# Low-rank products of four sequences at a time, with high halves and rests stacked in 128 rows

## The reference, cut to what matters

```python
# cond: B = 32 sequences, T = 32 tokens, rank R = 16
base_out = jnp.einsum('bti,oi->bto', x, W) + b
A = lora_As[adapter_mapping]          # per sequence: 512 x 16
Bm = lora_Bs[adapter_mapping]         # per sequence: 16 x 512
lora_h = jnp.einsum('bti,bir->btr', x, A)
lora_out = jnp.einsum('btr,bro->bto', lora_h, Bm)
xt = base_out + lora_out * 2.0
# ffn: router (softmax, 2 of 16 experts within 2 of 4 groups), experts, shared expert
y = sum over experts e: gate[:, e] * ((silu(xt @ w1 + b1) * (xt @ w2 + b2)) @ w3 + b3)
z = silu(xt @ sw1 + sb1) * (xt @ sw2 + sb2) @ sw3 + sb3
out = x + y + z
```

## Time and profile before

| | |
|---|---|
| median of three runs | 129.47 us (129.31 to 129.48) |
| profiled execution, its own time | 129.17 us |
| its span, first to last instruction | 127.3 us |
| mean granted TensorE clock | 1.000 |
| TensorE matmuls busy (815 instructions) | 123.3 us |
| TensorE weight loads busy (815) | 102.0 us |
| VectorE busy (195) | 86.4 us |
| ScalarE busy (84) | 47.8 us |

### The profile page before, as it was taken

One profiled execution on the slowest core, in us unless ns is written; L12 is line 12 of the kernel. 1 busy time (PEld: TensorE's weight loads), 2 busy tenths in 40 slices (PEclk: granted clock), 3 DMA queues, 4 the chain that ended last, 5 costly groups with the idle time before them and its releaser, 6 DMA issues.

```text
span 127.3 us, 2241 instructions
## 1 busy us (share of the span) xinstructions
PE 123.3 (97%) x815; PEld 102.0 (80%) x815; DVE 86.4 (68%) x195; ACT 47.8 (38%) x84; POOL 19.0 (15%) x33
## 2 busy tenths in 40 slices
PE   6999999999999999999999999999999999999991
PEld 6978867987789787888788889886888888888891
DVE  1659194257879859989999964456715379997631
ACT  1644473697529644007654654241014010000000
POOL 7364005000000020000057000033800000000000
PEclk9999999999999999999999999999999999999999
DMA  3999788669990699549007999994227999332222
GB/s 109 298 322 399 241 351 257 261 221 376 376 346 14 122 192 227 122 143 345 6 0 194 364 278 397 392 359 161 94 82 250 347 396 369 124 127 103 99 88 82
DMA packets 16908, 28.77 MB, mean 226 GB/s; under 512 B 1952, under 2 KB 6432, under 8 KB 16768
## 3 DMA queue, kind: packets, MB, share of 16 engines
q1 hardware_dynamic: 11728, 17.07, 40.5%
q10 hardware_dynamic: 3952, 7.34, 15.9%
q0 software_dynamic: 1216, 4.20, 10.3%
HBM read 19.17 MB, written 9.44 MB: 225 GB/s over the span
## 4 chain that ended last, share of the span: by engine, by line
PE 84%; DMA 6%; SPq 5%; ACT 2%; issue 1%; DVE 0%; ACTq 0%
PE bank L1002 61%; DMA xT_raw<-in_xT 6%; PE bank L1204 6%; PE bank L1061 5%; PE bank L1218 3%; SPq L319 2%; PE bank L1049 2%; PE bank L1279 2%; PE bank L1072 1%; PE bank L1194 1%; PE bank L1035 1%; ACT xT_h L462 1%; PE bank L1109 1%; PE bank L1179 1%; SPq L327 1%
## 5 line engine op out<-in xcount | busy, mean ns | idle before, releaser
L1002 PE MATMUL bank<-xtT_h,w12e_h 128*128 128x512 f32 x32 | 13.1, 409 | 0.0
L1002 PE MATMUL bank<-xtT_h,sw_h 128*128 128x512 f32 x32 | 12.9, 403 | 0.0
L1002 PE MATMUL bank<-xtT_l,sw_h 128*128 128x512 f32 x32 | 12.5, 391 | 0.0
L1002 PE MATMUL bank<-xtT_l,w12e_h 128*128 128x512 f32 x32 | 12.5, 391 | 0.0
L1002 PE MATMUL bank<-xtT_h,w12e_l 128*128 128x512 f32 x32 | 12.5, 391 | 0.0
L1002 PE MATMUL bank<-xtT_h,sw_l 128*128 128x512 f32 x32 | 12.5, 390 | 0.0
L975 DVE SCALAR_TENSOR_TENSOR x_sb<-rows_sb,val,x_sb 128x512 f32<-128x512 f32 x16 | 11.7, 747 | 0.2
L981 DVE TENSOR_TENSOR x_sb<-x_sb,bank 128x512 f32<-128x512 f32 (+1 forms) x9 | 5.6, 625 | 4.8 <-PE bank L1002 4.8
L799 DVE SCALAR_TENSOR_TENSOR heT_sb<-bank,b_dense,sg_sb 128x512 f32<-128x512 f32 x4 | 3.0, 750 | 7.7 <-PE bank L1002 7.7
L1204 PEld LDWEIGHTS bank<-xgT_sb,w_ring 128*128 128x128 f32 x64 | 7.5, 192 | 0.5 <-issue 0.5
L678 DVE TENSOR_TENSOR xT_l<-xT_raw,xT_h 128x512 fp32r<-128x512 f32 (+1 forms) x6 | 5.2, 867 | 3.9 <-ACT xT_h L462 3.8
(11 more groups left out here) (185 smaller groups left out, 292.0 us busy)
## 6 DMA issues: line engine op xcount, KB each, us to landing
y_rows<-zeros ACTq DMA_DIRECT2D x2, 2048.0 KB, 10.6
rows_sb<-y_rows SPq DMA_DIRECT2D x8, 512.0 KB, 7.3
xT_raw<-in_xT SPq DMA_DIRECT2D x8, 256.0 KB, 6.9
xt_rows<-xt_turned SPq DMA_DIRECT2D x8, 256.0 KB, 4.8
w_ring<-in_w_turned SPq DMA_DIRECT2D x4, 512.0 KB, 9.2
x_sb<-in_x SPq DMA_DIRECT2D x1, 2048.0 KB, 14.8
out<-x_sb ACTq DMA_DIRECT2D x7, 256.0 KB, 2.0
condW_raw<-in_condWT ACTq DMA_DIRECT2D x4, 256.0 KB, 5.1
```

The lines of the kernel that those rows point to most:

```text
L1002: mm = pe.matmul(out, a[p], b[q], start=(start and n == 0), stop=(stop and n == 2))
```

## The change

Each group is cut in two halves `h` of four sequences: 64 rank rows and 128 tokens. In `loraB_stack[:, g % 2, h]` the 64 rows of the half hold B's high half, and the other 64 rows hold its rest. `lhT_twice` holds the high half of the masked product in both sets of rows, `lhT_rest` the rest in the own rows, with zeros in the others. So one matmul over 128 rows gives high by high plus rest by high, and a second one gives the high by rest: two matmuls of 128 moving tokens for each half, four for a group and chunk, where three of 256 were.

The copies and rests of B are made for each half, in 64 partitions each (the rests written to the other 64 partitions). The mask has 128 columns (`lmask_half`, added up from `lmask` once); VectorE copies the high half to the own rows, ScalarE to the others (`move_lhT`), VectorE makes the rests. ScalarE's and VectorE's work on groups 0 and 1 of B is moved ahead of x's second half. GpSimd's gathers wait for the same work, counted in halves.

```diff
-        lhT_split = at(162, "lhT_h", [P, 2, GT], F32R), at(164, "lhT_l", [P, 2, GT], F32R)
-        loraB_split = at(168, "loraB_h", [P, 2, DIM], F32R), at(172, "loraB_l", [P, 2, DIM], F32R)
+        lhT_twice = at(162, "lhT_twice", [P, 2, 2, P], F32R)
+        lhT_rest = at(164, "lhT_rest", [P, 2, 2, P], F32R)
+        loraB_stack = at(168, "loraB_stack", [P, 2, 2, DIM], F32R)
...
# GpSimd, gather_lora
-                    pool.wait_ge(loraB_done, g - 1)
+                    pool.wait_ge(loraB_done, 2 * (g - 1))
...
# ScalarE, hi_loraB and hi_lhT (now move_lhT)
-                act.copy(loraB_split[0][:, g % 2], lora_raw[:, g % 2, DIM:2 * DIM]).then_inc(loraB_hi, 1)
+                for h, rows in enumerate(ROW_HALVES):
+                    act.copy(loraB_stack[rows, g % 2, h], lora_raw[rows, g % 2, DIM:2 * DIM]).then_inc(loraB_hi, 1)
...
-                act.copy(lhT_split[0][:, g % 2], lhT_sb[:]).then_inc(lhT_hi, 1)
+                for h, rows in enumerate(ROW_HALVES):
+                    act.copy(lhT_twice[ROW_HALVES[1 - h], g % 2, h], lhT_sb[rows, 0:P]).then_inc(lhT_moved, 1)
...
# ScalarE, order
+            hi_loraB(0)
+            hi_loraB(1)
             hi_xT(1, 0, 2)
             hi_xT(1, 2, 4)
-            hi_loraB(0)
             copy_loraA(0)
-            hi_loraB(1)
             copy_loraA(1)
-            hi_lhT(0)
-            hi_lhT(1)
+            move_lhT(0)
+            move_lhT(1)
...
# VectorE
             dve.memset(lhT_sb[:, 0:P], 0.0).then_inc(zeros_ready, 1)
+            then(dve.memset(lhT_rest[:].bitcast(F32), 0.0))
...
-                dve.wait_ge(loraB_hi, g + 1)
-                rest(loraB_split[1][:, g % 2], lora_raw[:, g % 2, DIM:2 * DIM], loraB_split[0][:, g % 2], loraB_done)
+                for h, rows in enumerate(ROW_HALVES):
+                    dve.wait_ge(loraB_hi, 2 * g + h + 1)
+                    rest(loraB_stack[ROW_HALVES[1 - h], g % 2, h], lora_raw[rows, g % 2, DIM:2 * DIM],
+                         loraB_stack[rows, g % 2, h], loraB_done)
...
# VectorE, mask_lh
                 if g >= 1:
-                    dve.wait_ge(lhT_done, g)
+                    dve.wait_ge(lhT_done, 2 * g)
+                    dve.wait_ge(lhT_moved, 2 * g)
                 dve.wait_ge(lh_done, g + 1)
-                quarters = "p (q t) -> p q t"
-                dve.tensor_tensor(lhT_sb[:].rearrange(quarters, q=QUARTER),
-                                  bank[5][:, 0:P // 2].unsqueeze(1).to_broadcast([P, QUARTER, P // 2]),
-                                  lmask[:].rearrange("p q r -> p (q r)").rearrange(quarters, q=QUARTER), ALU.mult
+                halves = "p (q t) -> p q t"
+                dve.tensor_tensor(lhT_sb[:, 0:P].rearrange(halves, q=2),
+                                  bank[5][:, 0:HALF_P].unsqueeze(1).to_broadcast([P, 2, HALF_P]),
+                                  lmask_half[:].rearrange("p q r -> p (q r)").rearrange(halves, q=2), ALU.mult
                                   ).then_inc(lh_masked, 1)
-                dve.wait_ge(lhT_hi, g + 1)
-                rest(lhT_split[1][:, g % 2], lhT_sb[:], lhT_split[0][:, g % 2], lhT_done)
+                if g >= 2:
+                    dve.wait_ge(cond_done, KC)
+                dve.wait_ge(lh_masked, g + 1)
+                for h, rows in enumerate(ROW_HALVES):
+                    dve.tensor_copy(lhT_twice[rows, g % 2, h], lhT_sb[rows, 0:P]).then_inc(lhT_hi, 1)
+                for h, rows in enumerate(ROW_HALVES):
+                    dve.wait_ge(lhT_hi, 2 * g + h + 1)
+                    rest(lhT_rest[rows, g % 2, h], lhT_sb[rows, 0:P], lhT_twice[rows, g % 2, h], lhT_done)
...
# VectorE, order
+            lo_lora(0)
+            lo_lora(1)
             lo_xT(1, 0, 2)
             lo_xT(1, 2, 4)
-            lo_lora(0)
-            lo_lora(1)
             dve.wait_ge(consts_ready, 5)
+            then(dve.tensor_tensor(lmask_half[:], lmask[:, 0:SEQ_PER_GROUP // 2], lmask[:, SEQ_PER_GROUP // 2:], ALU.add))
...
# TensorE, cond_lora
-                        pe.wait_ge(lhT_done, g + 1)
-                        pe.wait_ge(loraB_done, g + 1)
-                        at = g % 2 * GT
-                        for p, q in ((0, 0), (0, 1), (1, 0)):
-                            mm = pe.matmul(cond_bank(n, m)[:, at:at + GT], loraB_split[q][:, g % 2, m * P:(m + 1) * P],
-                                           lhT_split[p][:, g % 2, :], start=False, stop=(p == 1 and g % 2 == 1))
+                        pe.wait_ge(loraB_done, 2 * (g + 1))
+                        pe.wait_ge(lhT_moved, 2 * (g + 1))
+                        pe.wait_ge(lhT_done, 2 * (g + 1))
+                        for h in range(2):
+                            at = g % 2 * GT + h * P
+                            out, dims = cond_bank(n, m)[:, at:at + P], slice(m * P, (m + 1) * P)
+                            pe.matmul(out, loraB_stack[:, g % 2, h, dims], lhT_twice[:, g % 2, h], start=False, stop=False)
+                            mm = pe.matmul(out, loraB_stack[:, g % 2, h, dims], lhT_rest[:, g % 2, h],
+                                           start=False, stop=(h == 1 and g % 2 == 1))
                     mm.then_inc(cond_done, 1)
```

More of the change, by code:

```diff
@@ L25 @@
 GT = T // GROUPS_L
+HALF_P = P // 2
+ROW_HALVES = (slice(0, HALF_P), slice(HALF_P, P))
 E, INTER, SHARED = 16, 128, 256
@@ L152, in program @@
         lmask = sb("lmask", [P, SEQ_PER_GROUP, SEQ_LEN])
+        lmask_half = sb("lmask_half", [P, SEQ_PER_GROUP // 2, SEQ_LEN])
         tri16 = sb("tri16", [P, E, E])
@@ L227, in program @@
             sem("loraA_copied"), sem("xt_whole"), sem("loraB_hi"), sem("loraB_done"))
+        lhT_moved = sem("lhT_moved")
         first_hi, zeros_ready = sem("first_hi"), sem("zeros_ready")
@@ L477, in hi_loraB, with move_lhT @@
                     act.wait_ge(cond_done, KC)
-                act.copy(loraB_split[0][:, g % 2], lora_raw[:, g % 2, DIM:2 * DIM]).then_inc(loraB_hi, 1)
-            def hi_lhT(g):
+                for h, rows in enumerate(ROW_HALVES):
+                    act.copy(loraB_stack[rows, g % 2, h], lora_raw[rows, g % 2, DIM:2 * DIM]).then_inc(loraB_hi, 1)
+            def move_lhT(g):
                 act.wait_ge(lh_masked, g + 1)
@@ L534, in _ @@
             hi_sw12(1)
-            hi_lhT(2)
+            move_lhT(2)
             copy_lgT(0)
@@ L539, in _ @@
             exps(0)
-            hi_lhT(3)
+            move_lhT(3)
             for m in range(KC):
```

## The result

The changed kernel takes 135.76 us (median of four executions, 134.82 to 136.62) against 129.47 for the kernel before: ratio 1.046, 95% interval 1.042 to 1.050, some 6.3 us more. The forecast was 131.3. The ratios given here leave out executions over 1.5% above the fastest of the same kernel, some of which had only a lower clock of TensorE, while the medians are those of all executions.

A forecast was written before the change was run, and what follows sets the result against it. The prediction took TensorE's chain to bound the kernel, with its waits on ScalarE and VectorE. Its terms 0.35 + 0.66 + 0.80 gave +1.81 us, added to the shown median 129.47: 131.3 us, range 129.9 to 132.4.

The forecast's parts named there:

- ScalarE's new order: Ahead of x's second half, four `loraB` copies delay the first `copy_loraA`, for which TensorE waits: +0.35 us, bounds 0 to 0.6.
- The second block's stall: In the second `cond_lora` block TensorE waits 0.24 us at group 3 for VectorE's `mask_lh(3)`; bounds 0 to 0.55.
- the clock: TensorE's granted clock, full in every slice of the profile, was given no term in the sum.
- a worse chain: Rival: group 1 lands later or small operations cost more, delays together exceeding 1.2 us: 132.4 or more; chance 0.05.
- The bound: TensorE's matmuls bound the kernel; what one costs before 125 us arrives at the end more or less in full.
- The clock plays no part: Said of TensorE in the profile before the change, because the granted clock was full in every slice.
- TensorE's products: In `cond_lora`, 64 matmuls of 128 columns at 0.110 us replace 48 of 256: 7.04 against 5.82, +1.22 us.
- stream-bound rival: Weight loads overlap fully, a 128-column matmul costs 0.064 us, but a stall of 1.38 follows: 129.4 us; chance 0.09.
- half overlap: Rival: a 128-column matmul pitch midway, 0.087 us, with a 0.7 us stall: +0.8, 130.3 us; chance 0.06.
- The 81 ns of the Trainium skill: Skill's figure for a load and matmul of 128 columns in a stream; by it the time would be 130.0 us.
- The chain: VectorE's second-block work from `lo_sw12(0)` through `lo_lora(3)` to `mask_lh(3)`, which was to end near 38.60 us.
- 0.35, 0.66 and 0.80: The sum's terms: ScalarE's order, first `cond_lora` block (3.52 - 2.86), second block with its stall (3.52 + 0.24 - 2.96).

The follow-up runs named there:

- the second profile of before: The kernel before, unaltered, profiled once more; 129.29 us.
- the full-clock profile of the changed kernel: The changed kernel, unaltered, run again for its spread; the profiled execution took 133.42 us at granted clock 1.000.
- The waits-only run: The kernel before, products unchanged, with the new order of the first groups' rows and four unneeded VectorE memsets ahead of group 3's mask; 131.22 us.

## Why the prediction was wrong

**What failed, in short.** Three terms of the sum. ScalarE's new order was put at 0.35 us and cost 1.38. The second block's stall was put at 0.24 us and was 1.49. And the clock was put at nothing; its falls add 1.6 or 3.2 us. The first two are the forecast's own rival "a worse chain" (132.4 or more), which it gave a chance of 0.05 because "the landing is read directly from SyncE's 14.52". They alone take the kernel, at full clock, to 133.2 to 133.4 us, past the range's end at 132.4.

**The bound was right, the clock was not.** "The clock plays no part" held for the profile it was read from. The forecast made TensorE wait at two places and priced only the waits. In seven of ten executions of the changed kernel the clock fell, in all four behind the median of 135.76 us.

**TensorE's products: right.** 0.111 us for each of 64, in the first block 27.45 - 23.93 = 3.52 us as forecast, the load as the cause shown by halving either side. The stream-bound rival and half overlap are out. The 81 ns of the Trainium skill ("TensorE: Matmul & The Clock Gate", section "Back-to-back issue gap") does not hold for this fp32r stream, where it is 111. Its columns / 1.2 for a load (section "LDWEIGHTS (loading the stationary operand)") agrees, 107 against 111.

**ScalarE's order, +0.35: mis-sized.** Two causes. The landing of group 1 was read from one execution, the earliest of all seen; it came 0.9 us later. And two half copies take 1.26 us, 0.22 more than forecast. Between the second profile of before and the full-clock profile of the changed kernel `lora_h(0)` moves from 17.91 to 19.29, 1.38 us:

```profile
17.91 0.65 PE L1049 MATMUL bank<-xT_raw,loraA_sb 128*32 128x64 f32 x32 [1.01 <-ACT loraA_sb L472]
19.29 0.65 PE L1067 MATMUL bank<-xT_raw,loraA_sb 128*32 128x64 f32 x32 [2.29 <-ACT loraA_sb L477]
```

That the order alone, with whole copies, came out at 0.35 us in the timed runs does not bear the forecast out: in its profile group 1 landed at 16.3 us.

**The second block's stall, 0.24: the step that failed on VectorE.** The chain was right in every link, and each of its prices too low: `mask_lh(2)` and `mask_lh(3)` 1.5 us each (forecast 1.1 to 1.17), `lo_lora(3)` 1.33 instead of 1.21, `lo_sw12(1)` 1.25 instead of 1.14 between half operations. The stall is 1.49. These four are 0.95 of the 1.25 us that the forecast lacks; the rest was not taken apart.

**The sum at full clock.** From the second profile of before (span 127.5) to the full-clock profile of the changed kernel (131.7): first wait 1.38, first block 3.52 - 2.88 = 0.64, second block with its stall 5.03 - 2.96 = 2.07. That is 4.1 of 4.2 us. The forecast's terms were 0.35, 0.66 and 0.80.

**The clock: what is shown and what stays open.** Shown: with the same waits and work, an execution with the fall is 3.2 us longer; with the old products and no wait put in, no execution was longer for a low clock (the kernel before once shows a mean of 0.951 at its usual time, 129.54 us, and there is no profile of that); it fell behind waits of 2.0 and 1.9 us with no matmul of `cond_lora` before it, and once behind a loader-bound stream of 64 tokens without a new wait. Filling the second wait left it full four times of four. Not shown: why first waits of 1.9 to 2.4 us left it full in five profiles and lowered it in two, and how much of the changed kernel's seven falls in ten the 128-column stream adds to the wait of 1.3 us ahead of it; only one of the seven was profiled. The waits-only run bears on that, but its first wait came out shorter.

## What to carry to other kernels

Before making a matmul narrower, read the weight load's pitch from the loads' own durations at two widths; below that pitch, fewer columns save nothing, and each added load costs in full. Splitting an operation by partitions doubled its price here (one cast of 512 columns took 0.62 us over 128 partitions, two over 64 took 1.26), and took away the overlap between the halves. A wait that a change puts on TensorE is not priced by its length alone: a look at the granted clock by stretch, over several executions, belongs to it, as does more than one profile where a landing decides.

## What was not expected of the hardware

- One program on one core ran at three levels, 133.3, 134.9 and 136.5 us, and their mean granted clock tells them apart (1.000, 0.987, 0.973 to 0.975). In the one profile of the longest, TensorE ran at 1.2 GHz for 6.9 us behind the same wait that left it at 2.4 in the one of the shortest.
- Half-partition operations did not overlap: on ScalarE two of 0.62 us took 1.26 and the next operation began only then, where whole ones began 0.52 us apart; on VectorE two of 0.69 took 1.41.
- A gather at the same place of the program landed between 14.5 and 16.4 us from one execution to the next, with the DMA engines busy throughout from 10 to 14 us (0.98 in the changed kernel).
